# A four-layer graph network on one core: waits for the tile group a step reads, PSUM banks cleared by VectorE, one-scalar comparisons, and an earlier look-up

## The reference

```
edge_index = stack([src, dst])
# layer 0: attention;  h_msg, h_trans are linear in the nodes
exp_l   = exp(leaky(h_trans[src] @ a_src + h_trans[dst] @ a_dst))
h_neigh = segment_sum(exp_l / (denom[dst] + 1e-9) * h_msg[src], dst)
x = layernorm(x + leaky(x + h_neigh + (x * h_neigh) @ W2_w.T + W2_b))
# layer 1: four heads of attention with keys, values and an edge bias
# layer 2: message network, summed by the edge's SOURCE
e   = silu(silu(concat([h[src], h[dst]]) @ We1 + be1) @ We2 + be2)
agg = segment_sum(e, src);  x = layernorm(x + h + silu(concat([h, agg]) @ Wn1 + bn1) @ Wn2 + bn2)
# layer 3: two graph convolutions, with loops at every node
h   = relu(segment_sum((x @ W1)[src] * norm, dst) + b1)
out = segment_sum((h @ W2)[src] * norm, dst) + b2
return layernorm(x + out)
```

## Time and profile before

| | us |
|---|---|
| median of 3 runs | 5702.95 (5699.57 to 5705.49) |
| the profiled execution | 5707.85 |
| its span in the trace | 5706.1 |
| attention pass, first to last gather | 101.6 to 1174.4 |
| key and value pass | 1289.4 to 2331.3 |
| MLP pass | 2434.2 to 3427.7 |
| c1 | 3609.7 to 4597.1 |
| c2 | 4654.9 to 5635.9 |

### The profile page before, as it was taken

How to read it: one execution, slowest core, us unless ns; L and a number is a source line. 1 busy time by engine, 2 the same in 40 slices (tenths; PEclk the granted TensorE clock), 3 DMA queues, 4 the chain that set the end, 5 groups by cost and what they waited for, 6 DMA issues and landing times. The chain is left out here.

```text
span 5706.1 us, 80490 instructions
## 1 busy us (share of the span) xinstructions
PE 3351.8 (59%) x17155; PEld 2787.7 (49%) x17156; DVE 2996.6 (53%) x10412; ACT 1491.7 (26%) x5625; POOL 3889.4 (68%) x4054
## 2 busy tenths in 40 slices
PE   4444444366666666779999999444444454444443
PEld 3333333355655556667777777333333343333333
DVE  6887777577777787733333333333333343333335
ACT  2334333345555555511111113100000000000001
POOL 3777777727777777377777770577777747777773
PEclk7555555577788787855555556655555565655555
DMA  4222112224444444121111110111111121111111
GB/s 123 54 53 53 53 53 56 48 62 132 132 130 131 131 132 130 52 61 53 53 53 53 53 53 11 52 53 52 52 52 52 52 56 53 53 52 52 52 52 52
DMA packets 220198, 386.15 MB, mean 68 GB/s; under 512 B 83394, under 2 KB 119824, under 8 KB 219940
## 3 DMA queue, kind: packets, MB, share of 16 engines
q0 software_dynamic: 142944, 296.35, 19.0%
q1 hardware_dynamic: 76996, 86.71, 4.9%
HBM read 356.23 MB, written 26.56 MB: 67 GB/s over the span
## 5 line engine op out<-in xcount | busy, mean ns | idle before, releaser
L2187 POOL DMA_INDIRECT arena<-table_gcn,idx_now x1568 | 1491.1, 951 | 717.0 <-issue 418.4
L2234 PE MATMUL pair<-arena,hotf 128*128 x3328 | 755.6, 419 | 1095.3 <-DMA arena<-table_gcn,idx_now 1094.0
L2234 PEld LDWEIGHTS pair<-arena,hotf 128*128 128x128 f32 x3328 | 705.6, 322 | 1240.0 <-issue 1239.9
L655 POOL DMA_INDIRECT arena<-table_attention,idx_now x832 | 811.9, 976 | 271.1 <-issue 193.2
L655 POOL DMA_INDIRECT arena<-table_key_value,idx_now x832 | 788.7, 948 | 276.3 <-issue 220.6
L2261 DVE TENSOR_TENSOR acc<-acc,pair 128x1024 f32 x208 | 253.8, 1220 | 1342.5 <-PE pair L2237 1342.4
L1804 POOL DMA_INDIRECT arena<-table_edge_mlp,idx_now x784 | 754.9, 963 | 261.5 <-issue 214.0
L1043 PE MATMUL pair<-wide,hotf 128*128 128x130 f32 x1664 | 430.9, 439 | 630.4 <-ACT wide L1007 620.9
L1043 PEld LDWEIGHTS pair<-wide,hotf 128*128 128x128 f32 x1664 | 369.1, 326 | 695.5 <-ACT wide L1007 685.8
L2196 ACT COPY idx_now<-src_t 128x8 int32 (+1 forms) x204 | 39.3, 197 | 1876.9 <-PE pair L2237 1865.7
L1942 DVE TENSOR_TENSOR hot<-pair,arena 128x64 f32<-128x64 f32 x832 | 134.0, 224 | 640.0 <-DMA arena<-table_edge_mlp,idx_now 619.1
(11 more groups left out here) (366 smaller groups left out, 5586.6 us busy)
## 6 DMA issues: line engine op xcount, KB each, us to landing
key<-rel_dram SPq DMA_DIRECT2D x104, 256.0 KB, 3.5
arena<-rel_dram SPq DMA_DIRECT2D x52, 512.0 KB, 3.7
arena<-table_gcn,idx_now POOLq DMA_INDIRECT x1568, 2.5
arena<-table_attention,idx_now POOLq DMA_INDIRECT x832
arena<-table_key_value,idx_now POOLq DMA_INDIRECT x832
arena<-table_edge_mlp,idx_now POOLq DMA_INDIRECT x784, 2.4
table_attention<-arena SPq DMA_DIRECT2D x13, 512.0 KB, 2.9
table_gcn<-acc SPq DMA_DIRECT2D x26, 256.0 KB, 2.3
```

What stands on the lines that cost most here:

```text
L655: q_.indirect_dma_start(ring[:, slot, 0:width], None, table, bass.IndirectOffsetOnAxis(ap=idx_now[:, slot:slot + 1].bitcast(U32), axis=0)) ...
L2187: q_.indirect_dma_start(conv_ring[:, slot * D:(slot + 1) * D], None, table, bass.IndirectOffsetOnAxis(ap=idx_now[:, slot:slot + 1].bitcast ...
L2234: t_.matmul(window[:, bass.ds(offset * D, D)], hot8[:, g % 2, u, :], conv_ring[:, bass.ds(slot * D, D)], start=False, stop=False)
```

## The change

- **Waits.** A table gives for each step group the newest tile group that it reads: the edge tile of its last step divided by 8. It is computed beside the slot table, written to DRAM by a DMA of its own behind the slot table's (once in the setup, once in the attention pass), and read back, every eighth entry, in n2 and n3. POOL counts tile groups as landed in order: group k - 2 when it starts group k, group 96 in the middle of group 97, and 97 at the end. PE (c1, c2) and DVE (`before_silu`) load the table's entry into a register and wait for that count. The pass's waits for the tile group of the step group's own number go.
- **Banks.** Behind each addition DVE clears the window (`memset`, 128x1024 in c1 and c2, 128x512 in the MLP pass). PE waits for the clearing and then starts the accumulation with a zero matmul over 128 columns of each bank (64 in the MLP pass), which was 512. In c1 and c2 there are three windows instead of four. In the MLP pass the last product closes the sum, not a matmul of its own.
- **Look-up.** The seven DMAs stand ahead of the last 12 groups of gathers of the attention pass; decoding and transposing are done within the pass.
- **Last bias.** ACT copies it to a PSUM window that is free now; DVE adds it from there in 13 operations.
- **Comparisons.** One operation over 4 (attention pass) or 8 tiles (MLP pass, sums) with two inputs in SBUF becomes 4 or 8 `tensor_scalar` operations, each with one scalar per partition.

```diff
                     sp.dma_start(step_slot_dram.rearrange("(b p) -> p b", p=P), slot_i[:, :]).then_inc(slots_out, 16)
+                    sp.dma_start(step_need_dram.rearrange("(b p) -> p b", p=P), need_i[:, :]).then_inc(slots_out, 16)
...
+                dve.wait_ge(keys_done, 1)
+                ch(v.tensor_scalar(out=need_i[:, :], in0=put_i[:, :, :].rearrange("p a b -> p (a b)")[:, 0:SB], scalar1=3, scalar2=None,
+                                   op0=ALU.logical_shift_right))
...
-                    v.tensor_tensor(out=hotf[:, g, :, :], **hots(g))
+                    for u in range(G):
+                        v.tensor_scalar(out=hotf[:, g, u, :], in0=iota[:, :], scalar1=rel_now[:, g * G + u:g * G + u + 1], scalar2=None,
+                                        op0=ALU.is_equal)
...
                 pool.wait_ge(t0_out[0], 16 * ((NB + 1) // 2))
                 pool.wait_ge(t0_out[1], 16 * (NB // 2))
-                edge_rounds(pool, lambda i, g, past, left: gather(pool, i, g, past, t0, D + 2, l0_placed))
+                for g in range(RING):
+                    gather(pool, 0, g, g, t0, D + 2, l0_placed)
+                with pool.Fori(1, ITERS - 3) as i:
+                    for g in range(RING):
+                        gather(pool, i, g, RING, t0, D + 2, l0_placed)
                 pool.wait_ge(sort_steps, 1)
                 pool.wait_ge(sort_written, 16)
                 for b in range(SB):
                     at = bass.IndirectOffsetOnAxis(ap=put_i[:, :, :].rearrange("p a b -> p (a b)")[:, b:b + 1].bitcast(U32), axis=0)
                     q_.indirect_dma_start(key[:, b * P:(b + 1) * P], None, sorted_dram, at).then_inc(sort_got, 16)
+                for k in range(LOOKED_UP, GROUPS):
...
                     sp.dma_start(step2_slot_dram.rearrange("(b p) -> p b", p=P), slot_i[:, :]).then_inc(sort_out, 16)
+                    sp.dma_start(step2_need_dram.rearrange("(b p) -> p b", p=P), need_i[:, :]).then_inc(sort_out, 16)
...
+                with nc.allow_non_contiguous_dma(reason="one entry per group of steps"):
+                    sp.dma_start(step2_need, step2_need_dram[0:STEPS].rearrange("(one k u) -> one k u", one=1, u=CG)[:, :, CG - 1]).then_inc(n2_rows, 16)
...
-        def landed(pool, i, g, k):
+        def count_landed(pool, k, tiles_landed):
+
+            h = k % CRING
+            pool.wait_ge(conv_gathered[h], conv_count[h] + 16 * CG * (k // CRING + 1))
+            pool.sem_inc(tiles_landed, 1)
+
+        def landed(pool, i, g, k, tiles_landed):
 
             if not isinstance(k, int) or k >= 2:
                 h, j = (g - 2) % CRING, i - (1 if g < 2 else 0)
                 pool.wait_ge(conv_gathered[h], conv_count[h] + 16 * CG * (j + 1))
+                pool.sem_inc(tiles_landed, 1)
+            else:
+                pool.sem_inc(rounds, 1)
+
+        def rows_of(eng, need, table, k):
+
+            eng.reg_load([need], table[0:1, bass.ds(k, 1)])
+            return eng.snap(need, min_val=0, max_val=CTILE_GROUPS - 1) + 1
...
-                    landed(pool, i, g, k)
-                    pool.sem_inc(rounds, 1)
+                    landed(pool, i, g, k, l2_landed)
                     for u in range(CG):
                         slot = g * CG + u
+                        if isinstance(k, int) and k == CTILE_GROUPS - 1 and u == CG // 2:
+                            count_landed(pool, k - 1, l2_landed)
                         q_.indirect_dma_start(mlp_ring[:, slot * EH:(slot + 1) * EH], None, t2, bass.IndirectOffsetOnAxis(
                             ap=idx_now[:, slot:slot + 1].bitcast(U32), axis=0)).then_inc(conv_gathered[g], 16)
...
+                count_landed(pool, CTILE_GROUPS - 1, l2_landed)
...
-                    at_least(pe, l2_acc, k, -1)
-                    t_.matmul(window, zeros2[:, 0:P], zeros2, start=True, stop=False)
+                    pe.wait_ge(l2_clear, k + 1)
+                    t_.matmul(window[:, 0:EH], zeros2[:, 0:P], zeros2[:, 0:EH], start=True, stop=False)
                     pe.wait_ge(l2_same, k + 1)
                     pe.wait_ge(l2_s2, k + 1)
                     for u in range(CG):
                         offset = pe.snap(offsets[u], min_val=0, max_val=CG - 1)
-                        t_.matmul(window[:, bass.ds(offset * EH, EH)], hot8[:, g % 2, u, :], s2[:, g % 2, u * EH:(u + 1) * EH],
-                                  start=False, stop=False)
-                    t_.matmul(window[:, 0:2], zeros2[:, 0:P], zeros2[:, 0:2], start=False, stop=True).then_inc(l2_sum, 1)
+                        last = t_.matmul(window[:, bass.ds(offset * EH, EH)], hot8[:, g % 2, u, :], s2[:, g % 2, u * EH:(u + 1) * EH],
+                                         start=False, stop=(u == CG - 1))
+                    last.then_inc(l2_sum, 1)
...
-                    if not isinstance(k, int) or k < CTILE_GROUPS:
-                        dve.wait_ge(conv_gathered[g], conv_count[g] + 16 * CG * (i + 1))
+                    dve.wait_ge(l2_landed, rows_of(dve, need, step2_need, k))
...
-                    v.tensor_tensor(out=hot8[:, g % 2, :, :], in0=iota[:, :].unsqueeze(1).to_broadcast([P, CG, P]),
-                                    in1=rel_now[:, g * CG:(g + 1) * CG].unsqueeze(2).to_broadcast([P, CG, P]),
-                                    op=ALU.is_equal).then_inc(l2_same, 1)
+                    for u in range(CG):
+                        last = v.tensor_scalar(out=hot8[:, g % 2, u, :], in0=iota[:, :], scalar1=rel_now[:, g * CG + u:g * CG + u + 1], scalar2=None,
+                                               op0=ALU.is_equal)
+                    last.then_inc(l2_same, 1)
 
...
                     v.tensor_add(here, here, bank[6 + g % 2].rearrange("p (t f) -> p t f", t=CG)).then_inc(l2_acc, 1)
+                    if not isinstance(k, int) or k + 2 < CSTEP_GROUPS:
+                        dve.wait_ge(l2_acc, k + 1)
+                        v.memset(bank[6 + g % 2], 0.0).then_inc(l2_clear, 1)
...
+                for n in range(2):
+                    v.memset(bank[6 + n], 0.0).then_inc(l2_clear, 1)
...
-                        window = pair[g % 4]
+                        window = pair[g % 3]
                         pe.reg_load(slots, step_slot[0:1, bass.ds(k * CG, CG)])
                         pe.reg_load(offsets, step_offset[0:1, bass.ds(k * CG, CG)])
-                        at_least(pe, added, k, -3)
+                        pe.wait_ge(cleared, k + 1)
                         for h in range(2):
-                            t_.matmul(window[:, h * 512:(h + 1) * 512], zeros[:, 0:P], zeros, start=True, stop=False)
+                            t_.matmul(window[:, h * 512:h * 512 + D], zeros[:, 0:P], zeros[:, 0:D], start=True, stop=False)
                         pe.wait_ge(hot_made, k + 1)
-                        if not isinstance(k, int) or k < CTILE_GROUPS:
-                            pe.wait_ge(conv_gathered[g], conv_count[g] + 16 * CG * (i + 1))
+                        pe.wait_ge(tiles_landed, rows_of(pe, need, step_need, k))
...
-                        v.tensor_add(here, here, pair[g % 4][:, :].rearrange("p (t d) -> p t d", t=CG)).then_inc(added, 1)
+                        v.tensor_add(here, here, pair[g % 3][:, :].rearrange("p (t d) -> p t d", t=CG)).then_inc(added, 1)
+                        if not isinstance(k, int) or k + 3 < CSTEP_GROUPS:
+                            dve.wait_ge(added, k + 1)
+                            v.memset(pair[g % 3][:, :], 0.0).then_inc(cleared, 1)
...
+                    for n in range(3):
+                        v.memset(pair[n][:, :], 0.0).then_inc(cleared, 1)
                     front(0, 0)
-                    if also:
-                        also()
+                    if also_dve:
+                        also_dve()
...
+        last_bias = pair[3][:, 0:BT * D].rearrange("p (t d) -> p t d", t=BT)
+        bias_kept = sem("bias_kept")
+
+        def keep_last_bias():
+            s_.copy(last_bias, bg2[:, :].unsqueeze(1).to_broadcast([P, BT, D])).then_inc(bias_kept, 1)
+
         def add_last_bias():
-            v.tensor_tensor(out=xs[:, :, :], in0=xs[:, :, :], in1=bg2[:, :].unsqueeze(1).to_broadcast([P, NT, D]), op=ALU.add)
-
-        convolution("c1", t3, t3_out, add_last_bias)
+            v.wait_ge(bias_kept, 1)
+            for b in range(NB):
+                v.tensor_tensor(out=xs[:, four(b), :], in0=xs[:, four(b), :], in1=last_bias, op=ALU.add)
+
+        convolution("c1", t3, t3_out, keep_last_bias, add_last_bias)
```

77 lines of the change are left out of this document (52 added, 25 removed).

## The result

The changed kernel takes 5687.37 us (median of 9 runs) against 5704.94 of before: ratio 0.9968, 95% interval 0.9957 to 0.9978. It is 18 us faster (13 to 25 by the interval); 96 were forecast, with a range that ended at 5655. The profiled execution has a span of 5685.5, 20.6 less than before.

What follows compares the result with a forecast made beforehand. POOL's issuing of gathers, one every 1.25 us, was taken to bound the gather passes. The terms sum to -95.8: 5707.85 becomes 5612.0, and 5607 us as the execution lies 4.9 above the median; range 5572 to 5655.

Steps and rivals of the forecast that it cites:

- PSUM cleared by VectorE: MLP pass and convolutions: clears of 1.0 and 0.55 us lie off the path and hold no gather; 0 (0 to +138).
- The rival: MLP pass and convolutions: clearing PSUM holds gathers, by 142 us in all, giving 5749, slower than before; chance 0.05.
- MLP tail: Behind the MLP pass's last landing: waiting only for what is read leaves three step groups instead of six; -43.3 us.
- Scattered writes: Setup and attention pass: each need table's write of 896 small packets delays what follows; +10.4 us twice.
- held gathers of the attention pass: Attention pass: splitting the two-input comparison frees gathers that it held; -11 us, bounds 0 and -30.
- MLP comparison: MLP pass: one-scalar comparisons replace the two-input one that held gathers; -14 us, bounds 0 to -18.
- rival 2: Attention and MLP passes: one-scalar comparisons hold gathers too, giving 5639 us; chance 0.16, alone or with TensorE not keeping up.
- Convolution tails: Behind the last landings of c1 and c2: one step group left instead of seven; -21.7 and -20.5 us.
- Held gathers: c1, MLP and attention passes: gathers held by VectorE's two-input SBUF operations get shorter; -7.0, -14 and -11 us.
- the bias: c1: the bias comes from PSUM, so the second gather isn't held; -7.0 us (7.96 - 0.94).
- Rival 1: Setup and attention pass: the need tables' scattered writes cost little, giving 5586 us; chance 0.12.
- Look-up: Attention pass and behind it: gathers issued earlier cost POOL the same 8.7 us, only decoding goes; -0.5 us, 0 to -3.

Runs made afterwards that it cites:

- e5: Changed kernel with a register mask before each count wait, VectorE clearing no bank and zero matmuls of 512 columns back: 5616.17 us, 0.984 of before.
- e16: As e5, but in c1 and c2 VectorE also does a 128x1024 memset into unread SBUF: between 7063.68 and 7078.34 us, in the stalled sets.
- e8: Changed kernel with the attention pass's comparison as one two-input operation again: 5661.7 us, 0.9921 of before.
- e17: As e6, with the attention pass's comparison as one two-input operation again: 5603.9 us, 0.9824 of before.
- e6: As e5, but in both convolutions step group 103 waits for tile group 97's gathers themselves and POOL doesn't count that group: 5614.32 us, 0.9841 of before.
- e18: As e17, with the two need tables placed behind all other tables in DRAM: 5616.66 us, 0.9847 of before.
- the stalled sets: Three sets of follow-up runs in which the kernel before the change took 6955 to 6971 us.
- e3: Kernel before plus VectorE's bank clearing, narrower zero matmuls and three windows, waits and all else unchanged: 6974 us, 1.0008 of before, in the stalled sets.

## Why the prediction failed, point by point

**The step that failed** is "PSUM cleared by VectorE": "as the operations that touch PSUM don't, I put 0". The row I leaned on the earlier trace rows was of an addition over the same window, and what counts is the operation, not the memory: a memset with a comparison right behind it holds a gather that starts within it. Cost: 70 us under clearings (22.9 + 23.1 + 23.6), and e5 without them is 71 us faster. The clearings themselves took 0.91 and 0.48 us, where I had 1.0 and 0.55. The rival had the mechanism, with 5% chance and twice the hold. Its argument that clearings fall into step with the gathers was right: 139 of the 202 in the convolutions have a gather starting 0.6 to 0.7 us behind their own start, which makes the holds many and short.

That e5, at 5616 us, lies 9 us from my 5607 is in part luck: without the clearings the other terms miss, as the changed kernel's trace has them, by -13 (MLP tail), -9 and -9 (scattered writes), +25 (held gathers of the attention pass), +4 (MLP comparison) and +7 (closing drain), which nearly cancel.

The Trainium skill, page "SBUF — State Buffer", section "Who interferes with whom", says that a VectorE instruction with at most one SBUF input, outside the two-port modes, doesn't contend with GpSimd, and names a memset into SBUF as an exception only for the newer chip. The 13 gathers that start within an MLP clearing with nothing right behind it, none of them held, agree with that. With a comparison right behind it a memset, which has no input, holds gathers here, on trn2, whether it writes SBUF (e16) or PSUM; the measurement decides. The Trainium skill's sentence on tensor_scalar in that section, my rival 2, is borne out where an operation is bf16: gathers that start within the bf16 comparison of the MLP pass are held for 6.1 us in e5 (49 of 76), while the float32 ones hold 0.09 us on average where they hold at all.

**MLP tail**: -55.9 for -42.6. The mechanism is right; the size off by the moment of counting. I let POOL count group 95 when it starts group 97. But its instructions are taken up well ahead of the gathers:

```profile
3438.01 1.27 DVE L1991 TENSOR_TENSOR hot<-pair,arena 128x64 f32<-128x64 f32 x8 [5.05 <-POOLq L1819]
```

Step group 100, which needs group 95, is released at 3438.01. The last gather of group 95 starts at 3435.51 and the first of group 96 at 3436.76, so the release comes as group 95 lands. Group 97 starts at 3447.41: 9.4 us sooner than I had it.

**Convolution tails**: last additions 22.7 us (c1) closer to the last gather, as forecast; then 3.7 lost in each to the wait for POOL's closing drain (VectorE's pause behind the last addition is 4.02 us instead of 0.32 in c1), which I had not seen, since in the kernel before it lay under the 22 us of the tail.

**Held gathers**: the bias right (c1's second gather is short, and e5's c1 is 6.1 us shorter than before). MLP comparison: -14 forecast; its stretch fell from 15.1 to 5.3, so -10. Attention pass: -11 forecast, the stretch rose by 13.7. The term counted the hold that goes and not the ones that the moved instructions make; e8 against the change and e17 against e6 show it as 8 to 12 us the wrong way.

**Scattered writes**: +10.4 twice, measured +1.5 (VectorE goes on at 56.71 instead of 55.22) and a second gap of 5.08 us instead of 3.33. Rival 1 was right on the time here; the reason it gave was not tested, and the place of the tables decides too: e18 shows my price in the setup, 9.8 us against e17 to the first gather, and most of it in the attention pass, a gap of 12.12 us where I had said some 13.

**Look-up**: as forecast, -0.3 for -0.5.

## What to carry to other kernels

An engine that only issues DMAs is still slowed by what another engine does beside it, so an edit that gives idle VectorE a new kind of instruction has to be costed by that kind's own hold, and by what stands in its shadow. If no row shows the instruction, a chance of 5% for its worst case is too small where it is repeated 300 times. A tail that gets shorter uncovers what the tail had covered: look at what every engine does at the stage's end before counting the whole tail as gain.

## What the runs showed of the hardware

- A VectorE memset of 128x1024 float32 (0.91 us) with a comparison right behind it holds an indirect DMA that starts on POOL within it (192 of 196 in the changed kernel, 95 of 102 in e16), whether it writes PSUM or SBUF; ScalarE's copy (1.0 us) and VectorE's multiplication in PSUM (1.23 us) don't. A memset of 128x512 with nothing right behind it held none of 13.
- POOL takes up its instructions ahead of the gathers' execution, so a semaphore that it raises "at the start of a group" came 9.4 us sooner than that group.
- POOL's closing drain of the MLP pass and the convolutions ends 9.2 us behind the last gather's end (c1 of the kernel before, e6) or behind POOL's last wait, where that is later (the changed kernel).
- The same scattered write of 896 packets landed in 10.8 or 18.4 us, by where its table lies in DRAM.
- In the stalled sets register operations of TensorE's sequencer took 0.7 us instead of 0.03 to 0.08, and engines stood idle for some 5 us behind work that was done. The key and value pass, whose code is the same in all kernels, took 1390 us there in e3 and 1417 to 1436 in those with the need tables and the moved look-up, 1040 to 1043 elsewhere. e18 was to tell why and ran in an undisturbed set; it stays open.
